# Two small-head attentions: values projected once and spread over blocks by DMA, exponentials weighed unnormalised

## The reference

```python
# L0_xattn, q = layernorm(x)                       # L1_attn, x = layernorm(x)
qp = q @ Wq.T                                      # q = x Wq + bq      (16 heads)
k, v = split(latent_kv @ Wkv_expand.T)             # k, v = x Wk + bk, x Wv + bv   (4 groups, each for 4 heads)
scores = einsum('bhqd,bhkd->bhqk', qh, kh) / 4     # the same
scores = where(causal, scores, min)                # the same
attn = softmax(scores); out = einsum('bhqk,bhkd->bhqd', attn, vh)
return out @ Wout.T                                # out is returned as it is
```

## Time and profile before

| | |
|---|---|
| runs of the kernel | 1296.14, 1305.05, 1308.14 us |
| profiled execution, first to last instruction | 1311.3 us |
| PE, PEld busy | 1228.9, 948.2 us |
| DVE, ACT, POOL busy | 772.9, 525.3, 224.2 us |
| first small attention | 20 to 158 us |
| second small attention | 973 to 1110 us |

### The profile page before, as it was taken

How to read it: one execution, slowest core, us unless ns; L and a number is a source line. 1 busy time by engine, 2 the same in 40 slices (tenths; PEclk the granted TensorE clock), 3 DMA queues, 4 the chain that set the end, 5 groups by cost and what they waited for, 6 DMA issues and landing times. The chain is left out here.

```text
span 1311.3 us, 33068 instructions
## 1 busy us (share of the span) xinstructions
PE 1228.9 (94%) x12845; PEld 948.2 (72%) x12846; DVE 772.9 (59%) x1978; ACT 525.3 (40%) x1507; POOL 224.2 (17%) x293
## 2 busy tenths in 40 slices
PE   3999899999999889999979999999989998899997
PEld 1777688788888668987957777777658886646664
DVE  3788755444554565553257888888858998302221
ACT  0666454334433312221045555565526664112221
POOL 0500000000000000000145455554300000132222
PEclk9999999999999989999589999999998998799999
DMA  8200000000000066000002111112164000122221
GB/s 260 98 0 0 1 1 1 0 0 0 0 0 0 1 178 159 0 0 14 20 11 51 51 40 34 48 49 50 38 226 158 0 0 32 44 76 39 39 45 14
DMA packets 53673, 58.27 MB, mean 44 GB/s; under 512 B 12140, under 2 KB 45548, under 8 KB 52968
## 3 DMA queue, kind: packets, MB, share of 16 engines
q1 hardware_dynamic: 49528, 53.14, 14.3%
q0 software_dynamic: 4080, 4.22, 1.6%
HBM read 47.85 MB, written 10.40 MB: 44 GB/s over the span
## 5 line engine op out<-in xcount | busy, mean ns | idle before, releaser
L1520 ACT ACTIVATE xattn_exps<-xattn_ps_s,xattn_top 128x256 f32<-128x256 f32 x256 | 118.0, 475 | 77.6 <-DVE xattn_top L1588 77.6
L601 PEld LDWEIGHTS attn_ps_q<-attn_xnT,w_b_q 128*128 128x128 f32 x1024 | 118.8, 193 | 12.6 <-issue 12.6
L601 PE MATMUL attn_ps_q<-attn_xnT,w_b_q 128*128 128x128 f32 x1024 | 123.4, 276 | 0.0
L655 PE MATMUL attn_ps_out<-w_b_o,attn_oT 128*128 128x256 f32 x480 | 106.5, 380 | 1.8 <-DVE all_x L836 1.5
L655 PEld LDWEIGHTS attn_ps_out<-w_b_o,attn_oT 128*128 128x128 f32 x480 | 90.0, 190 | 15.1 <-DVE all_x L836 2.4
L709 ACT COPY attn_qT<-attn_ps_q 128x512 f32<-128x512 f32 x64 | 38.0, 594 | 148.2 <-PE attn_ps_q L601 148.2
L1087 POOL TENSOR_TENSOR fold_last_cos<-raw_last,all_consts 64x64 f32<-64x64 f32 x1 | 0.3, 312 | 563.2 <-POOLq L899 563.2
L1595 DVE STREAM_TRANSPOSE xattn_expsT<-xattn_exps 128x1024 f32<-128x1024 f32 x64 | 79.4, 1241 | 20.4 <-ACT xattn_exps L1520 20.4
L1585 DVE TENSOR_REDUCE xattn_raw_top<-xattn_ps_s 128x4 f32<-128x1024 f32 x64 | 77.8, 1216 | 15.8 <-PE xattn_ps_s L1412 15.7
L1412 PE MATMUL xattn_ps_s<-xattn_kT,xattn_qT 64*32 64x256 f32 x2048 | 70.0, 383 | 3.2 <-ACT xattn_exps L1520 3.2
L1422 PE MATMUL xattn_ps_o<-xattn_expsT,xattn_kv 32*64 32x256 f32 x2048 | 63.5, 380 | 4.6 <-DVE xattn_last_scores L1631 3.9
(11 more groups left out here) (318 smaller groups left out, 2611.2 us busy)
## 6 DMA issues: line engine op xcount, KB each, us to landing
xattn_inverse<-xattn_inverse_rows SPq DMA_DIRECT2D x30, 256.0 KB, 4.1
all_c<-in_ctx SPq DMA_DIRECT2D x64, 64.0 KB, 1.8
moe_gate<-in_f_gate SPq DMA_DIRECT2D x8, 512.0 KB, 7.8
moe_up<-in_f_up SPq DMA_DIRECT2D x8, 512.0 KB, 7.6
moe_down<-in_f_down SPq DMA_DIRECT2D x8, 512.0 KB, 9.5
sorted_x<-all_zeros SPq DMA_DIRECT2D x1, 2944.0 KB, 14.2
experts_x_in<-sorted_x SPq DMA_DIRECT2D x23, 128.0 KB, 2.3
all_x<-in_x SPq DMA_DIRECT2D x4, 512.0 KB, 9.3
```

The source lines that it names most:

```text
L601: last = nc.tensor.matmul(ps_q[g % 2][:, h * P:(h + 1) * P], wq[:, c, head * DH:(head + 1) * DH], xnT[u][:, c, :], start=(c == 0), stop=(c ...
L655: last = nc.tensor.matmul(bank[:, 0:DIM], of_heads[:, h, :, :].rearrange("p b q -> p (b q)"), wo[:, h, :], start=(h == 0), stop=(h == HEAD ...
L1520: nc.scalar.activation(exps[g % 2][:, nkeys * k:nkeys * (k + 1)], ps_s[g % 2][:, nkeys * k:nkeys * (k + 1)], ACT.Exp, bias=top[u][:, n:n + ...
```

## The change

Both attentions change in the same way.

- Keys and values are made from each token once. In the first attention the context stands in both halves of the partitions, so that two key products and two value products use different rows of PE; in the second, four key products and two value products a tile.
- The values go to `v_rows`, token-major, in rows of 4 groups x 17: 16 values and a one, which POOL writes once. ACT copies them in the first attention, DVE adds the bias and writes them in the second.
- `v_blocks` is zeroed once by POOL. For each tile SP issues sixteen DMAs, SBUF to SBUF, each of 32 partitions x 68 numbers (272 bytes a partition), one for each batch and head of a group. `v_in[u]` counts them, and PE waits for all sixteen before it weighs.
- The exponentials aren't normalised first. They are turned, used as the stationary side, and the products give token-major rows whose 17th column of each head is the sum. DVE inverts it and scales the output (`outs_ready`), one step later than before.
- In the first attention the output is turned (two transposes more) before the last projection, and there is one step more at the end; in the second the transposes back to token-major are gone.
- The loads that SP issued in the background go to POOL's queue (`load_and_scale`, `load_ups_and_downs`). In the second attention POOL also makes the normalised x of every tile, behind these loads in its list.
- In the earlier FFN phase, SP lays out the value bias by two small DMAs and a broadcast.

```diff
@@ -195,53 +197,72 @@
...
+    vd = HD + 1
+    own = PER if cross else 1
...
+
+        @block.sync
+        def _(sp):
+            sp.wait_ge(blank, 4)
+            for t in range(TILES):
+                u = t % 2
+                sp.wait_ge(v_ready, t + 1)
+                wait_count(sp, o_made, t - 1)
+                for b in range(TB):
+                    for r in range(PER):
+                        sp.dma_start(v_blocks[u][SEQ * r:SEQ * r + SEQ, b, r, :, :], v_rows[u][SEQ * b:SEQ * b + SEQ, r % own, :, :])\
+                          .then_inc(v_in[u], 16)
+
+        @block.gpsimd
+        def _(pool):
+            for u in range(2):
+                nc.gpsimd.memset(v_blocks[u][:, :, :, :, :], 0.0).then_inc(blank, 1)
+                nc.gpsimd.memset(v_rows[u][:, :, :, HD], 1.0).then_inc(blank, 1)
+            if beside:
+                beside(pool)
+            if not cross:
+                for t in range(TILES):
+                    if t == TILES - 1:
+                        pool.wait_ge(dve_roots, Moments.LAST_LINKS)
+                    wait_count(pool, turned, t)
+                    nc.gpsimd.tensor_scalar(xn[:, :], x_sb[:, t, :], moments.moments[:, t, 0:1], moments.factors[:, t:t + 1],
+                                            ALU.subtract, ALU.mult).then_inc(xn_ready, 1)
 
...
-            def keys_queries(t, u):
+            def keys_values(t, u):
                 pe.wait_ge(xnT_ready, t + 1)
-                for m in range(KC):
-                    for c in range(kchunks):
-                        nc.tensor.matmul(ps_k[:, m * P:(m + 1) * P], w["k"][0:kin, c, m * P:(m + 1) * P],
-                                         srcT[u][0:kin, c, :, 0, :], start=(c == 0), stop=(c == kchunks - 1))
+                wait_count(pe, v_ready, t)
+                if cross:
+                    halves = (slice(0, CTX), slice(CTX, 2 * CTX))
+                    for m, rows in enumerate(halves):
+                        nc.tensor.matmul(ps_k[m], w["k"][rows, 0, m * P:(m + 1) * P], ctxT[u][rows, :], start=True, stop=True)
+                    for m, rows in enumerate(halves):
+                        last = nc.tensor.matmul(ps_v[m], ctxT[u][rows, :], w["v"][rows, 0, m * P:(m + 1) * P], start=True, stop=True)
+                else:
+                    for m in range(KC):
+                        for c in range(KC):
+                            nc.tensor.matmul(ps_k[m], w["k"][:, c, m * P:(m + 1) * P], xnT[u][:, c, :],
+                                             start=(c == 0), stop=(c == KC - 1))
+                    for c in range(KC):
+                        last = nc.tensor.matmul(ps_v[0], xnT[u][:, c, :], w["v"][:, c, :], start=(c == 0), stop=(c == KC - 1))
+                last.then_inc(kv_made, 1)
+
...
-            def values(t, u):
-                wait_count(pe, v_ready, parts * t)
-                for n in range(TB // parts):
-                    for half in range(parts):
-                        b = parts * n + half
-                        rows = slice(kin * half, kin * half + kin) if cross else slice(0, P)
-                        for c in range(kchunks):
-                            last = nc.tensor.matmul(ps_values[half][:, n * vw:(n + 1) * vw],
-                                                    srcT[u][rows, c, b, :, :].rearrange("p r k -> p (r k)"),
-                                                    w["v"][rows, c, :], start=(c == 0), stop=(c == kchunks - 1))
-                last.then_inc(v_made, 1)
+                last.then_inc(q_made, 1)
...
-                            last = nc.tensor.matmul(ps_scores[p][rows, m * P:(m + 1) * P], kT[half, m, rows],
-                                                    q_blocks[half, m, b, :, :].rearrange("p h q -> p (h q)"),
-                                                    start=False, stop=True, skip_group_check=True)
+                            last = nc.tensor.matmul(ps_scores[rows, 512 * p + m * P:512 * p + (m + 1) * P], kT[half, m, rows],
+                                                    q_blocks[half, m, :, rows], start=False, stop=True, skip_group_check=True)
...
+            def turn_exps(t):
+                pe.wait_ge(exps_ready, t + 1)
+                if cross:
+                    wait_count(pe, x_ready, t - 1)
                 for g in range(GROUPS):
-                    last = nc.tensor.transpose(ps_pT[:, g * P:(g + 1) * P], probs[:, g * P:(g + 1) * P], ident)
-                last.then_inc(probs_turned, 1)
+                    last = nc.tensor.transpose(ps_pT[:, g * P:(g + 1) * P], exps[:, g * P:(g + 1) * P], ident)
+                last.then_inc(exps_turned, 1)
 
             def weigh(t, u):
-                pe.wait_ge(v_ready, parts * (t + 1))
-                pe.wait_ge(probsT_ready, t + 1)
-                wait_count(pe, x_ready, t)
+                pe.wait_ge(v_in[u], 128 * t + 256 - 128 * u)
+                pe.wait_ge(expsT_ready, t + 1)
+                wait_count(pe, o_ready, t)
                 for g in range(GROUPS):
                     m, p = g // 2, g % 2
-                    half = slice(64 * p, 64 * p + 64)
                     for b in range(TB):
-                        at = ((p * KC + m) * TB + b) * SEQ
-                        last = nc.tensor.matmul(ps_o[half, m * P + b * SEQ:m * P + (b + 1) * SEQ],
-                                                v_blocks[u][:, b * GROUPS + g, :, :].rearrange("p h d -> p (h d)"),
-                                                probsT[:, at:at + SEQ], start=True, stop=True)
+                        at = (p * KC + m) * P + b * SEQ
+                        last = nc.tensor.matmul(ps_o[b * SEQ:(b + 1) * SEQ, g * PER * vd:(g + 1) * PER * vd],
+                                                expsT[:, at:at + SEQ], v_blocks[u][:, b, :, g, :], start=True, stop=True)
                 last.then_inc(o_made, 1)
 
...
+            def turn_outs(t, turned_tiles):
+                pe.wait_ge(o_ready, t + 1)
+                pe.wait_ge(xnT_ready, turned_tiles)
+                flat = outs[:, :, :].rearrange("p h d -> p (h d)")
+                for c in range(KC):
+                    last = nc.tensor.transpose(ps_oT[:, c * P:(c + 1) * P], flat[:, c * P:(c + 1) * P], ident)
+                last.then_inc(o_turned, 1)
...
             def step(i, u, live):
                 if live(0):
                     scores(i)
                 if live(-1):
-                    turn_probs(i - 1, live(0))
-                if live(1):
-                    keys_queries(i + 1, 1 - u)
+                    turn_exps(i - 1)
+                if cross and live(-2):
+                    turn_outs(i - 2, i + 2 if live(1) else TILES)
+                if live(1):
+                    keys_values(i + 1, 1 - u)
+                    queries(i + 1, 1 - u)
+                if cross and live(-2):
+                    finish(i - 2, i if live(-1) else TILES)
                 if live(2):
                     turn(i + 2)
                 if live(-1):
                     weigh(i - 1, 1 - u)
-                if live(1):
-                    values(i + 1, 1 - u)
...
+            def values_out(t, u):
+                wait_count(act, v_in[u], 128 * t - 128 * u)
+                for m in range(KC):
+                    groups = slice(m * GROUPS // 2, (m + 1) * GROUPS // 2)
+                    last = nc.scalar.copy(v_rows[u][:, :, groups, 0:HD].rearrange("p r g d -> p g r d"),
+                                          ps_v[m].rearrange("p (g r d) -> p g r d", g=GROUPS // 2, r=PER))
                 last.then_inc(v_ready, 1)
 
...
+            def values_out(t, u):
+                dve.wait_ge(kv_made, t + 1)
+                wait_count(dve, v_in[u], 128 * t - 128 * u)
+                nc.vector.tensor_tensor(v_rows[u][:, 0, :, 0:HD], ps_v[0].rearrange("p (g d) -> p g d", g=GROUPS),
+                                        w["bv"][:, :].rearrange("p (g d) -> p g d", g=GROUPS), ALU.add).then_inc(v_ready, 1)
+
+            def outs_ready(t):
+                dve.wait_ge(o_made, t + 1)
                 s2.tile(t)
-                s2(nc.vector.reduce_sum(total[:, :], exps[:, :, :], axis=X_AXIS))
-                s2(nc.vector.reciprocal(inverse[:, :], total[:, :]))
+                s2(nc.vector.reciprocal(inverse[:, :], o_view[:, :, HD]))
                 s2.end()
-                wait_count(dve, probs_turned, t)
-                nc.vector.tensor_tensor(probs[:, :].rearrange("p (h k) -> p h k", h=HEADS), exps[:, :, :],
-                                        inverse[:, :].unsqueeze(2).to_broadcast([P, HEADS, SEQ]), ALU.mult).then_inc(probs_ready, 1)
+                if cross:
+                    wait_count(dve, o_turned, t)
+                nc.vector.tensor_tensor(outs[:, :, :], o_view[:, :, 0:HD], inverse[:, :].unsqueeze(2).to_broadcast([P, HEADS, HD]),
+                                        ALU.mult).then_inc(o_ready, 1)
 
             def residual(t):
-                dve.wait_ge(out_made, t + 1)
```

(54 more changed lines are left out.)

210 lines of the change are left out of this document (79 added, 131 removed).

## The result

The changed kernel takes 1407.50 us (median of 4 runs, 1404.21 to 1409.62) against 1305.65 us for the kernel before (4 runs, 1296.14 to 1308.14): a ratio of 1.0788, 95% interval 1.0744 to 1.0833. The prediction was 1338 us with a range of 1298 to 1380. The direction and the place were right, the size was 70 us short.

What follows compares the result with a forecast made beforehand. SP's issues were to pace both attentions and POOL's loads to delay the second: 6.7 + 26.9 - 1.3 + 1 = +33.3 us, giving 1338 us against the median of 1305.05. The range was 1298 to 1380.

Steps and rivals of the forecast that it cites:

- What bounds the new kernel: Both attentions: SP's sixteen issues a tile, 7.86 us with waits, set the pace above PE's 6.35 and 6.1 us.
- The SP term: Both attentions: 0.485 us from issue to issue on SP, sixteen in 7.76 us, 7.86 us a tile with waits.
- The bound of 0.60: Upper bound for one SP issue, from an issue from SBUF lasting 0.55 us and a gap of 0.05.
- First attention, +6.7: First attention: 16 tiles at SP's 7.86 us and a longer end, last addition at 163.9 instead of 157.2 us.
- POOL ahead of the second, +26.9: Before the second attention: POOL's clearing, sixteen loads (24 us) and normalising delay the start from 973.6 to 1000.5 us.
- The rival of POOL paying per row: Loads before the second attention cost 61 us instead of 24, by rows or a full queue: 1375 us; chance 0.15.
- The rival of cheap issues: POOL's loads before the second attention take 7.8 us instead of 24: 1322 us, or 1316 at 2 us; chance 0.12.
- The rest of the second, -1.3 and +1: Second attention from its first normalised tile: 133.6 us against 134.9 (-1.3), and +1 for PE starting at its lower clock.
- PE's step, 6.35 and floor 6.1: PE's step in the first attention 6.35 us; the second's floor 6.1 us, with DVE's work and handovers.
- SP keeps up: Both attentions: issues of 0.40 us or less hide and PE paces, 1295 us, turning point 0.42 us; chance 0.17.
- PE's clock falls: Attention steps: waiting lowers PE's clock, a step takes 10.8 us; for a quarter of 32 steps +24, 1362 us; chance 0.08.

Runs made afterwards that it cites:

- one write, four reads: Changed kernel, each tile's values written to HBM in one transfer and read back in four, replacing sixteen SBUF to SBUF transfers: 1257.30 us.
- one load a tile: Kernel with one write and four reads a tile, second attention's POOL normalising first, then clearing, and issuing one weight load behind each tile: 1242.60 us.
- two queues: Changed kernel with eight of each tile's sixteen SBUF to SBUF transfers issued by SP and eight by POOL: 1282.90 us.
- half of the transfers: Changed kernel with eight of the sixteen transfers a tile left out, their blocks keeping a constant: 1259.85 us.
- loads two tiles later: Kernel with one write and four reads a tile, POOL normalising two tiles before the second attention's sixteen loads: 1260.02 us.
- sixteen out of HBM: Changed kernel with its sixteen transfers a tile read from HBM, where the first tile's values were put once: 1333.57 us.
- the test of single issues: Kernel before, with groups of sixteen scratch DMAs added in a later phase, twelve forms on SP, three on POOL: 1305.63 us in one run.

## Why the prediction was wrong, point by point

- **What bounds the new kernel: right.** SP's issues stand one behind the other in both attentions and PE waits for `v_blocks` before it weighs.
- **The SP term: this step failed.** "I take the 32-partition row, since only the bytes in each row differ." The bytes make no difference indeed, but the route did differ: the row is a load out of HBM, the change moves SBUF to SBUF, and no SP issue of the kernel before has both ends in SBUF. Measured 0.644 and 0.646 us for 0.485, that is 39.0 and 39.6 us more over the two attentions. The bound of 0.60 didn't hold it either: its row, 0.55, is one write into HBM, not a row of this route, and sixteen such writes in a row took only 0.42 us each above, so it bounded nothing. With both mis-sized parts of the sum as measured, issues and POOL, it comes to 33.3 + 78.6 - 12.4 = +99.5; the attentions show +100.9.
- **First attention, +6.7:** +47.5. Besides SP's 39.0, the first rows of values came 1.5 us later than worked out (SP starts at 32.99, not 31.5: the first key products stand at 31.43 and not at 29.89), and the end took 0.3 more.
- **POOL ahead of the second, +26.9:** the mechanism was right, nothing hides it, and PE waits. The size was 15.0 us of work where I had 27.4: clearing 2.0, loads 11.8 for the 24 of the forecast, the first normalised tile 1.24. I had taken each load as nearest to the indirect DMA, 1.26 us; a direct load was 0.74, and hardly tied to its rows. The rival of POOL paying per row is refuted. The rival of cheap issues is nearer: 11.8 us for its 7.8. The Trainium skill, DMA: Bandwidth & Descriptors, section Anatomy of one DMA, says "You can emit a lot of descriptors before the incremental cost shows up", by which the issues would be nearly free. The trace agrees on the rows of one load (0.72 us for 256, 0.75 for 512) and not on the number of loads: 0.74 us each is not free, and spacing them out brought 14.7 us together with the clearing.
- **The rest of the second, -1.3 and +1:** SP's 39.6 us on top of these; the ends agree within 1.5 us.
- **PE's step, 6.35 and floor 6.1:** too large. Unhindered it is 5.15 us in the first attention (one write, four reads). Weighing takes 0.62 us from start to start where I had 1.10 (83.67 to 84.29), and two masks with the sixteen score products 0.92 (84.29 to 85.21) where I had carried 1.56 over. The second attention's step, by POOL's tiles above (955.53 to 960.85), is 5.3 us; there PE waits 0.7 us of each for DVE's query blocks, so DVE has a part in this step, as the prediction had it. This error cost the forecast nothing, since SP hid it, but it hid the size of the prize: with few issues and the loads spaced, this form of the attentions is worth 66 us (1242.60 against 1308.49, the kernel before beside it).
- **SP keeps up** was the rival on the other side, with a turning point of 0.42 us an issue. It fell for the change as made, and its mechanism is what the versions with fewer issues show.
- **PE's clock falls:** it did, 0.83 and 0.75 against 1.00 and 0.97 before, more than I had allowed for (chance 0.08 for well under 0.95 in the first). It cost little by itself, since a step of PE's at the lower level still fitted into SP's 10.3 us (3.27 us of waiting were left in the step shown).
- **Not foreseen, not settled:** the phases between the attentions, which the change touches only by two small DMAs, took 10.4 us less in the profiled execution of the changed kernel (mean clock 0.97 against 0.96). From the last residual of the first attention to the first work of the second, the traces with the change's phases between give 805.6 us (the changed kernel), 806.8 and 806.9 (one load a tile; one write and four reads), 807.2 (two queues), 808.2 (half of the transfers), 810.7 (loads two tiles later) and 813.0 (sixteen out of HBM); those without it give 816.0 and 810.6 (the test of single issues, with its DMAs in them). So executions whose phases between are the same code differ by 7.4 us and more than half of the 10.4 may be that; whether the change has a part in the rest stays open.

## What to carry to other kernels

When a change puts many small DMAs on one queue, price an issue by a row with the same route, source and destination both, and not by one with the same shape; where the trace has none, say that the bound is open and reach further. On a queue that issues without a pause the number of issues is what costs: one read that serves four batches replaced four transfers, and even with a write to HBM and a wait ahead of the reads this gave back 150 us. Here 74 us of that came with the route and 76 with the number, where PE's own step became the limit. A row of loads ahead of the first tile of a phase was paid in full, moving the row behind two tiles gained nothing, and one load a tile cost nearly nothing.

## What the runs showed of the hardware that was not expected

- On SP, an issue with both ends in SBUF took 0.57 to 0.60 us (median), one with an end in HBM 0.42 to 0.45, whatever the rows, the bytes and the partitions in the forms tried. On POOL the same SBUF to SBUF form took 0.51 us, less than on SP, and a form four times as large out of HBM 0.55.
- POOL issued 512 KB loads at 0.72 us each with 256 rows and 0.75 with 512.
- From the issue of a small write to HBM to SP's next read, which waits for it, it was 6.17 us while the sixteen 512 KB loads were under way (start of the second attention, sixteen transfers out of HBM), and 2.10 us in a step of the first attention (one write, four reads).
